# A mixture-of-experts stage whose token lists are made earlier and whose shared MLP is packed into three products instead of four

## The chip, the cores and the metric

One NeuronCore of a Trainium2 chip runs the kernel; the metric is the device time of one execution in microseconds (us), lower is better. TensorE (PE), VectorE (DVE), ScalarE (ACT), GpSimd (POOL) and SyncE (SP) each take their own instructions in program order and wait for each other by semaphores.

## The reference, cut to what matters

The program is a two-layer block over x of 32 batches of 128 tokens of 128 features: attention, an expert layer with 64 experts, attention with a bias, an expert layer with 8 experts. The change touches the first expert layer only. With xf the 4096 normalised tokens:

```python
scores = softmax(xf @ gate_w.T)
_, idx = top_k(scores + gate_b, 6)                # 6 of 64 experts
# each expert takes its first 64 tokens (CAP = 64) of a sorted list
h  = silu(einsum('ecd,eid->eci', xb, w1)) * einsum('ecd,eid->eci', xb, w3)
yb = einsum('eci,edi->ecd', h, w2)                # inner width 88
y  = zeros_like(xf).at[tok].add(contrib * wf[:, None])
z  = silu(xf @ ws1.T) * (xf @ ws3.T) @ ws2.T      # shared MLP, inner width 176
return y + z
```

## The kernel before, in words

The stage is `experts0_block`. It runs between the two attention stages, from about 279 to 388 us of the span. It handles the 64 experts in NG = 8 groups g of GE = 8, and the shared MLP in NB = 8 blocks b of four batches (512 tokens). The order of the work on each engine is written out by hand, as calls of small helpers, and one pass of `for g in range(NG)` is called a turn here.

Helpers on TensorE. `running_counts` and `FIRST` count, with bf16 products, how many tokens each expert has got so far. `picks(n)` (L1204) multiplies kept counts `cumb` by a 0/1 matrix `tile_of`, for half of a group, into the bank PICK; it waits for `l_tiles` of its group (n // 2 + 1), for `l_cumb`, and until DVE has counted what the bank held before. `hidden(b, c)` (L1214) makes the inner rows of the shared MLP: for each half c of 88 inner rows one product of `ws1` and one of `ws3`, each 88x512. `project(b)` (L1226) multiplies by `ws2`. `places(g)` (L1237) transposes the gathered token rows, `expert_hidden(g)` (L1247) makes the 16 inner products of the group's experts, `outputs(g)` (L1259) its eight output products.

On ScalarE, `silu` (L1301) serves the shared MLP, L1310 copies the transposed rows (`xpT`), L1314 is the experts' own silu. On VectorE, `tiles(g)` (L1353 to L1358) builds `tile_of` of a group and releases `picks`, `keep_counts(j)` (L1344) fills `cumb`, `count(n)` (L1369) reads PICK and sums, `tokens(g)` (L1375) turns the sums of a group into addresses, `weights_and_rows(g)` (L1391 to L1395) takes the weights and row numbers out of the gathered rows, `gated(b, half)` (L1329) and L1434 multiply by the silu, `add_shared(b)` (L1334) adds the shared result, `scale(g)` (L1402) weights the experts' outputs. On GpSimd, `fetch(g)` (L1161) issues four indirect DMAs that gather the token rows of a group, `place(g)` (L1172) four that scatter its results. GpSimd's order is fetch(0), fetch(1), and then in turn g: fetch(g + 2), place(g). SP loads the experts' weights.

Lists are made LISTS = 3 groups ahead: in turn g VectorE runs `tiles(g + 3)` right after `weights_and_rows(g)`, and TensorE the two `picks` of that group, one behind `hidden(g + 2, 0)` and one behind `hidden(g + 2, 1)`. The shared MLP is AHEAD = 2 blocks ahead. The turn's first part on TensorE reads

```python
places(g)
if g + AHEAD - 1 < NB:
    project(g + AHEAD - 1)
expert_hidden(g)
if g + AHEAD < NB:
    hidden(g + AHEAD, 0)
if g + LISTS < NG:
    picks(2 * (g + LISTS))
outputs(g)
```

The weights of the shared MLP come with the list `later` in `setup_block`, whose loads SP issues at L403 near 17 us.

Of the kernel before, what the change touches and what calls it, by code (L numbers as in the profile page):

```python
# [178 lines left out]
def setup_block(nc, t, d, sem, ps):  # L179
# [14 lines left out]
        (t.wvT[1], d.wvT1), (t.woT[1], d.woT1), (t.wrT, d.wrT), (t.hs, d.hs), (t.ws13T, d.ws13T), (t.ws2T, d.ws2T),  # L194
# [897 lines left out]
def experts0_block(nc, t, d, sem, ps):  # L1092
# [26 lines left out]
    LISTS = 3  # L1119

# [12 lines left out]
    def pair(n):  # L1133
        return H1[n % 2], H3[n % 2]
# [6 lines left out]
    with nc.Block(no_gpsimd_drain=True) as block:  # L1141
# [45 lines left out]
        def _(pe):  # L1187
# [21 lines left out]
            def hidden(b, c):  # L1209
                n = use(b, c)  # L1210
                free(pe, n)
                rhs = t.XT[:, T4 * b:T4 * b + T4, :].rearrange("p k q -> p (k q)")
                for k, bank in enumerate(pair(n)):
                    mm = nc.tensor.matmul(bank[0:I0, :], t.ws13T[:, (2 * k + c) * I0:(2 * k + c + 1) * I0], rhs,  # L1214
                                          start=True, stop=True)
                mm.then_inc(s_h, 1)

            def project(b):
                if b == 0:
                    pe.wait_ge(l_cumb, 3)  # L1220
                else:
                    pe.wait_ge(s_zadd, b)
                pe.wait_ge(s_u, 2 * b + 2)
                for k in range(T4):
                    for c in range(2):
                        mm = nc.tensor.matmul(Z[:, D * k:D * k + D], t.uT[:, c, S * k:S * k + S],  # L1226
                                              t.ws2T[:, c, :], start=(c == 0), stop=(c == 1))
                mm.then_inc(s_z, 1)
# [39 lines left out]
            hidden(0, 0)  # L1268
            picks(0)
            picks(1)  # L1270
            pe.wait_ge(l_cumb, 1)
            hidden(0, 1)
            hidden(1, 0)
            picks(2)
            picks(3)
            project(0)
            hidden(1, 1)
            picks(4)
            picks(5)
            for g in range(NG):  # L1280
                places(g)
                if g + AHEAD - 1 < NB:
                    project(g + AHEAD - 1)
                expert_hidden(g)
                if g + AHEAD < NB:
                    hidden(g + AHEAD, 0)
                if g + LISTS < NG:
                    picks(2 * (g + LISTS))
                outputs(g)
                if g + AHEAD < NB:  # L1290
                    hidden(g + AHEAD, 1)
                if g + LISTS < NG:
                    picks(2 * (g + LISTS) + 1)

        @block.scalar
        def _(act):
            def silu(b, c):
                n = use(b, c)
                act.wait_ge(s_h, 2 * b + c + 1)
                free(act, n)  # L1300
                nc.scalar.activation(t.silu[:, n % 2, :], pair(n)[0][0:I0, :], ACT.Silu).then_inc(s_e, 1)  # L1301

            for b in range(AHEAD):
                silu(b, 0)
                silu(b, 1)
            for g in range(NG):
                act.wait_ge(r_T, g + 1)
                if g >= 2:
                    act.wait_ge(r_h, g - 1)
                nc.scalar.activation(t.xpT[:, g % 2, :], TP[:, :], ACT.Copy).then_inc(r_Tc, 1)  # L1310
                n = last_uses[g]
                act.wait_ge(r_h, g + 1)
                free(act, n)
                nc.scalar.activation(t.silu[:, n % 2, :], pair(n)[0][0:I0, :], ACT.Silu).then_inc(r_e, 1)  # L1314
                if g + AHEAD < NB:
                    silu(g + AHEAD, 0)
                    silu(g + AHEAD, 1)

        @block.vector
        def _(dve):  # L1320
# [3 lines left out]
            def gated(b, half):  # L1324
# [4 lines left out]
                ve.tensor_tensor(t.uT[:, half, :], pair(n)[1][0:I0, :], t.silu[:, n % 2, :], ALU.mult).then_inc(s_u, 1)  # L1329
# [84 lines left out]
            counted_tokens(0)  # L1414
            gated(0, 0)
            gated(0, 1)
            keep_counts(2)
            tiles(1)
            keep_counts(3)
            counted_tokens(1)  # L1420
            tiles(2)
            gated(1, 0)
            gated(1, 1)
            add_shared(0)
            counted_tokens(2)
            for g in range(NG):
# [5 lines left out]
                if g >= 2:  # L1432
                    dve.wait_ge(r_y, g - 1)
                ve.tensor_tensor(t.gT[:, g % 2, :], pair(n)[1][0:I0, :], t.silu[:, n % 2, :],  # L1434
                                 ALU.mult).then_inc(r_u, 1)
# [12 lines left out]
            c.end()  # L1448
# [422 lines left out]
def flamingo_kernel(nc, **dram):  # L1871
# [41 lines left out]
    with ExitStack() as ctx:  # L1913
# [27 lines left out]
        with ExitStack() as ex0:  # L1941
            t.ws13T = tile(ex0, "ws13T", [4 * I0], F32)
            t.gateT = tile(ex0, "gateT", [E0], F32)
            t.wrT = tile(ex0, "wrT", [E1], F32)
            t.silu = tile(ex0, "silu", [2, 512], F32, I0)
            t.uT = tile(ex0, "uT", [2, 512], F32, I0)
            t.gT = tile(ex0, "gT", [2, 512], F32, I0)
            t.ws2T = tile(ex0, "ws2T", [2, D], F32, I0)
# [199 lines left out]
```

## Time and profile before

| | |
|---|---|
| median of 3 runs | 928.5 us (928.15 to 934.57) |
| span of the profiled execution | 930.0 us |
| TensorE busy in the span | 716.6 us (77%) |
| VectorE busy | 691.5 us (74%) |
| GpSimd busy | 615.0 us (66%) |
| mean granted TensorE clock | 0.910 |

The runs' list does not say which of them was profiled. The span lies 1.5 us above the median; steps are worked out on the span and carried over to the median as differences. In a timeline row the two numbers in front are start and duration in us, and the bracket at the end gives the engine's idle time before the row and what ended it. A merged row (x16) starts with its first instruction. A matmul of f32 shows as two records.

### The profile page before, as it was taken

The page shows a single profiled execution, that of the slowest core. Times are in us where ns is not written, and L with a number is a line of the kernel's source. Part 1 is how long each engine was busy: PE and PEld are TensorE (multiplying, and loading weights), DVE is VectorE, ACT ScalarE, POOL GpSimd, SP SyncE. Part 2 cuts the span into 40 slices and gives each one's busy share as a digit, 9 for nine tenths or more (in the row PEclk, how much of TensorE's full clock was granted, in tenths as well). Part 3 has the DMA queues.
Part 4 walks back from the last instruction along what each step waited for, and adds up shares of the span by engine and source line. Part 5 has one row for each costly group of instructions (what it writes and reads, how often), then busy time and mean ns, then how long its engine had stood idle before and what let it go on. Part 6 is the DMA issues. An engine that isn't in the chain of part 4 may idle for free. (4 is left out here: it accounts for less than half of the span.)

```text
span 930.0 us, 23773 instructions
## 1 busy us (share of the span) xinstructions
PE 716.6 (77%) x6259; PEld 491.8 (53%) x6259; DVE 691.5 (74%) x2257; ACT 473.2 (51%) x1687; POOL 615.0 (66%) x1109
## 2 busy tenths in 40 slices
PE   3888999999947998258999999999711379879770
PEld 1555566556623666236666666666501256567550
DVE  3787999999966664148999999999878756765334
ACT  2886888888831222037777777777500033423220
POOL 4888666666643676467888888887300466777772
PEclk9999999999977999679999999999955599999895
DMA  5211222222113333134344434443100216655568
GB/s 164 77 50 69 78 76 78 79 79 92 71 59 102 105 105 104 47 103 136 126 145 134 132 124 139 143 143 106 59 9 1 81 48 173 179 163 166 163 180 240
DMA packets 98731, 100.61 MB, mean 108 GB/s; under 512 B 24511, under 2 KB 76077, under 8 KB 98659
## 3 DMA queue, kind: packets, MB, share of 16 engines
q1 hardware_dynamic: 88306, 88.25, 30.5%
q0 software_dynamic: 6656, 9.66, 3.7%
q10 hardware_dynamic: 3696, 1.84, 0.7%
q8 instruction: 32, 0.52, 0.2%
q14 instruction: 41, 0.33, 0.1%
HBM read 60.84 MB, written 44.17 MB: 113 GB/s over the span
## 5 line engine op out<-in xcount | busy, mean ns | idle before, releaser
L574 ACT ACTIVATE P<-bank,mx 128x120 f32<-128x120 f32 x1024 | 277.5, 430 | 70.3 <-DVE mx L876 70.3
L473 PE MATMUL bank<-ident,P 128*120 128x128 f32 x1024 | 167.2, 286 | 28.7 <-ACT P L574 24.0
L473 PEld LDWEIGHTS bank<-ident,P 128*120 128x120 f32 x1024 | 106.1, 138 | 116.7 <-issue 70.7
L876 DVE TENSOR_REDUCE mx<-bank 128x4 f32<-128x480 f32 x256 | 150.3, 649 | 21.2 <-PE bank L455 18.1
L1761 POOL DMA_INDIRECT xg<-token_rows,tokens x64 | 66.8, 1044 | 70.8 <-DVE tokens L1815 51.9
L446 PE MATMUL bank<-bp,identr 128*128 128x480 f32 x256 | 87.5, 428 | 0.0
L1771 POOL DMA_INDIRECT expert_sums<-y,sum_rows x64 | 72.8, 1137 | 22.2 <-issue 19.2
L491 PE MATMUL bank<-PT,Vb 120*32 120x128 f32 x2048 | 82.9, 280 | 5.1 <-DVE PT L884 4.5
L676 POOL TENSOR_TENSOR Km<-Kf,kmask 128x480 f32<-128x480 f32 x64 | 63.2, 987 | 28.2 <-ACT Kf L558 27.4
L641 POOL TENSOR_TENSOR rstd<-rs,minus_half 128x1 f32<-128x1 f32 x128 | 73.1, 571 | 10.7
L455 PE MATMUL bank<-Km,qf 32*128 32x480 f32 x512 | 70.9, 623 | 3.0 <-POOL Km L676 2.9
L884 DVE TENSOR_SCALAR PT<-bank,kept 120x512 f32<-120x512 f32 x96 | 67.5, 729 | 0.2 <-PE bank L473 0.2
L1743 ACT ACTIVATE ge<-bank,b1x 128x512 f32<-128x512 f32 x64 | 44.0, 687 | 45.6 <-PE bank L1695 45.6
L1707 PE MATMUL bank<-w2x,ge 128*128 128x128 f32 x512 | 67.1, 288 | 0.0
L1736 ACT ACTIVATE xgT<-bank 128x512 f32<-128x512 f32 x16 | 8.9, 595 | 113.9 <-PE bank L1684 113.9
L640 POOL TENSOR_SCALAR rs<-mv 128x1 f32<-128x1 f32 x128 | 29.1, 227 | 54.8 <-DVE mv L852 54.7
L491 PEld LDWEIGHTS bank<-PT,Vb 120*32 120x32 f32 x2048 | 48.6, 109 | 30.3 <-DVE PT L884 17.6
L1707 PEld LDWEIGHTS bank<-w2x,ge 128*128 128x128 f32 x512 | 63.7, 202 | 1.4 <-issue 1.4
L582 ACT ACTIVATE PT<-bank 120x512 f32<-120x512 f32 x64 | 41.6, 650 | 44.7 <-PE bank L473 44.7
L1695 PE MATMUL bank<-xgT,w1x 128*128 128x512 f32 x128 | 58.6, 611 | 0.0
L882 DVE COPY PT<-bank 120x512 f32<-120x512 f32 x64 | 43.0, 672 | 10.6 <-PE bank L473 10.3
L1161 POOL DMA_INDIRECT xp<-token_rows,place_tok x32 | 33.0, 1030 | 25.4 <-DVE place_tok L1375 16.6
(244 smaller groups left out, 1678.7 us busy)
## 6 DMA issues: line engine op xcount, KB each, us to landing
expert_sums<-zeros SPq DMA_DIRECT2D x32, 512.0 KB, 3.4
choice_rows<-zeros SPq DMA_DIRECT2D x32, 384.0 KB, 2.4
yrows<-choice_rows SPq DMA_DIRECT2D x32, 384.0 KB, 3.1
XT<-expert_sums SPq DMA_DIRECT2D x16, 512.0 KB, 6.3
XS<-expert_sums SPq DMA_DIRECT2D x16, 512.0 KB, 6.1
w<-in_w13T SPq DMA_DIRECT2D x8, 704.0 KB, 4.2
token_rows<-payload SPq DMA_DIRECT2D x32, 128.0 KB, 1.7
ctx<-in_ctxT SPq DMA_DIRECT2D x64, 60.0 KB, 2.0
```

What stands on the lines that cost most here:

```text
L446: nc.tensor.matmul(heads(SC[r]), t.identb[:] if L == 0 else t.identr[:], part.unsqueeze(1).broadcast_to([S, G, KV]), start=(x == 0), stop= ...
L455: nc.tensor.matmul(heads(SC[r]), t.qf[rows, u, :], t.Km[rows, u, :, :], start=False, stop=True).then_inc(ev.scores, 1)
L473: mm = nc.tensor.transpose(TB[r % 2][0:KV, S * j:S * j + S], t.P[:, r, j, :], t.ident[:])
L491: mm = nc.tensor.matmul(pv_ps[32 * j:32 * j + 32, S * (r // 2):S * (r // 2) + S], t.Vb[0:KV, v, 2 * j + r // 2, 32 * (r % 2):32 * (r % 2) ...
L574: e = nc.scalar.activation(t.P[:, r, j, :], heads(SC[r])[:, j, :], ACT.Exp, bias=t.mx[:, G * r + j:G * r + j + 1], scale=-1.0)
L641: power = nc.gpsimd.tensor_tensor(t.rstd[:, k, u, :], t.rs[:, k, u, :], t.minus_half[:], ALU.pow)
L676: nc.gpsimd.tensor_tensor(t.Km[:, w, :, :], t.Kf[:, w, :].unsqueeze(1).broadcast_to([D, G, KV]), t.kmask[:].unsqueeze(2).broadcast_to([D, ...
L876: ve.tensor_reduce(t.mx[:, G * r:G * r + G], heads(SC[r]), AX.X, ALU.min).then_inc(ev.mins, 1)
L884: ve.tensor_scalar(t.PT[0:KV, r, :], TB[r % 2][0:KV, :], at_col(t.kept, i), None, ALU.mult).then_inc(ev.pt_dve, 1)
L1707: mm = nc.tensor.matmul(Y[s][:, D * k:D * k + D], t.ge[:, s, c, 128 * k:128 * k + 128], t.w2x[:, e % 2, c, :], start=(c == 0), stop=(c == ...
L1761: nc.gpsimd.indirect_dma_start(out=t.xg[:, e % 2, k, :], out_offset=None, in_=d.rows_flat, in_offset=bass.IndirectOffsetOnAxis(ap=t.tokens ...
L1771: nc.gpsimd.indirect_dma_start(out=d.sums_flat, out_offset=bass.IndirectOffsetOnAxis(ap=t.sum_rows[:, e, k:k + 1], axis=0), in_=t.y1[:, e ...
```

## The change

Three parts, all in or for `experts0_block`.

First, the packing. The 176 inner rows of the shared MLP are cut into 128 and 48 instead of 88 and 88. `hidden(b, 0)` makes 128 rows of ws1 and 128 of ws3, `hidden(b, 1)` makes the other 48 of both in a single product of 112 rows (the second 48 at row 64). `silu`, `gated` and `project` follow; the second `gated` reads rows 64 to 111 and writes rows 0 to 47. The loads of `ws13T` and `ws2T` become seven DMAs instead of two.

Second, the start. The lists of groups 0, 1 and 2 are made ahead of most of the shared MLP, on TensorE and on VectorE.

Third, the turn. `project(g + 1)` moves behind `expert_hidden(g)`, `hidden(g + 2, 0)` behind `outputs(g)`, the first `picks` of a turn to a place between `places(g)` and `expert_hidden(g)`, the second between the two `hidden`. VectorE's `count`, `scale` and `gated` are put in another order in the turn; `tiles(g + 3)` stays behind `weights_and_rows(g)`.

```diff
-        ... (t.ws13T, d.ws13T), (t.ws2T, d.ws2T),
+        (t.ws13T[:, 0:128], d.ws13T[:, 0:128]), (t.ws13T[:, 128:256], d.ws13T[:, SI:SI + 128]),
+        (t.ws13T[:, 256:320], d.ws13T[:, 128:192]), (t.ws13T[:, 320:368], d.ws13T[:, SI + 128:2 * SI]),
+        (t.ws2T[0:I0, 0, :], d.ws2T[:, 0, :]), (t.ws2T[I0:128, 0, :], d.ws2T[0:128 - I0, 1, :]),
+        (t.ws2T[0:SI - 128, 1, :], d.ws2T[128 - I0:I0, 1, :]),
...
+    REST, UP = SI - 128, 64
...
-                for k, bank in enumerate(pair(n)):
-                    mm = nc.tensor.matmul(bank[0:I0, :], t.ws13T[:, (2 * k + c) * I0:(2 * k + c + 1) * I0], rhs,
+                if c == 0:
+                    for k, bank in enumerate(pair(n)):
+                        mm = nc.tensor.matmul(bank[:, :], t.ws13T[:, 128 * k:128 * k + 128], rhs, start=True, stop=True)
+                else:
+                    mm = nc.tensor.matmul(pair(n)[0][0:UP + REST, :], t.ws13T[:, 256:256 + UP + REST], rhs,
...
             for g in range(NG):
                 places(g)
+                if g + LISTS < NG:
+                    picks(2 * (g + LISTS))
+                expert_hidden(g)
                 if g + AHEAD - 1 < NB:
                     project(g + AHEAD - 1)
-                expert_hidden(g)
+                outputs(g)
                 if g + AHEAD < NB:
                     hidden(g + AHEAD, 0)
                 if g + LISTS < NG:
-                    picks(2 * (g + LISTS))
-                outputs(g)
+                    picks(2 * (g + LISTS) + 1)
                 if g + AHEAD < NB:
                     hidden(g + AHEAD, 1)
-                if g + LISTS < NG:
-                    picks(2 * (g + LISTS) + 1)
```

VectorE's queue in a turn (the one line that stays, `tiles`, is left in to show its place):

```diff
                 weights_and_rows(g)
                 if g + LISTS < NG:
                     tiles(g + LISTS)
...
                                  ALU.mult).then_inc(r_u, 1)
+                if g + LISTS < NG:
+                    count(2 * (g + LISTS))
                 if g + AHEAD - 1 < NB:
                     add_shared(g + AHEAD - 1)
+                scale(g)
                 if g + AHEAD < NB:
                     gated(g + AHEAD, 0)
-                scale(g)
-                if g + LISTS < NG:
-                    count(2 * (g + LISTS))
-                if g + AHEAD < NB:
-                    gated(g + AHEAD, 1)
                 if g + LISTS < NG:
                     count(2 * (g + LISTS) + 1)
                     tokens(g + LISTS)
+                if g + AHEAD < NB:
+                    gated(g + AHEAD, 1)
```

TensorE before, one turn (g = 1), from the transposes on; `tile_of` is the 0/1 matrix that `tiles` makes:

```order
548 L1237 MATMUL bank<-ident,xp 128x128 [waits mlp_places_T_copied,rows_fetched1]
549 L1237 MATMUL bank<-ident,xp 128x128 x3
550 L1226 MATMUL bank<-ws2T,uT 128x128 [waits mlp_gated,mlp_added]
551 L1226 MATMUL bank<-ws2T,uT 128x128 x7
552 L1247 MATMUL bank<-xpT,w 88x64 [waits mlp_weights_loaded1,mlp_places_T_copied,mlp_gated]
553 L1247 MATMUL bank<-xpT,w 88x64 x15
554 L1214 MATMUL bank<-XT,ws13T 88x512 [waits mlp_gated]
555 L1214 MATMUL bank<-XT,ws13T 88x512
556 L1204 MATMUL bank<-cumb,tile_of 128x129 [waits list_counted,list_counts_kept,list_tiles]
557 L1204 MATMUL bank<-cumb,tile_of 128x129
558 L1259 MATMUL bank<-w,gT 64x128 [waits mlp_expert_scaled,mlp_out_weights_loaded1,mlp_expert_gated]
```

The same turn in the changed kernel, whose line numbers are larger (L1246 is the transposes, L1209 `picks`, L1256 `expert_hidden`, L1235 `project`, L1268 `outputs`, L1220 `hidden(b, 0)`):

```order
545 L1246 MATMUL bank<-ident,xp 128x128 [waits mlp_places_T_copied,rows_fetched1]
546 L1246 MATMUL bank<-ident,xp 128x128 x3
547 L1209 MATMUL bank<-cumb,tile_of 128x129 [waits list_counted,list_counts_kept,list_tiles]
548 L1209 MATMUL bank<-cumb,tile_of 128x129
549 L1256 MATMUL bank<-xpT,w 88x64 [waits mlp_weights_loaded1,mlp_places_T_copied,mlp_gated]
550 L1256 MATMUL bank<-xpT,w 88x64 x15
551 L1235 MATMUL bank<-ws2T,uT 128x128 [waits mlp_gated,mlp_added]
552 L1235 MATMUL bank<-ws2T,uT 128x128 x7
553 L1268 MATMUL bank<-w,gT 64x128 [waits mlp_expert_scaled,mlp_out_weights_loaded1,mlp_expert_gated]
554 L1268 MATMUL bank<-w,gT 64x128 x7
555 L1220 MATMUL bank<-XT,ws13T 128x512 [waits mlp_gated]
```

The `picks` with its wait on `list_tiles` has moved ahead of `expert_hidden`, and `project` and `outputs` now stand between `expert_hidden` and the next `hidden`.

VectorE in the changed kernel, from the first `gated` of block 3 in turn 1 to `tile_of` of turn 2; L1341 and L1343 are the two `gated`, L1384 `count`, L1390 `tokens`, L1406 to L1410 `weights_and_rows`, L1368 to L1373 `tiles`:

```order
487 L1341 TENSOR_TENSOR uT<-bank,silu 128x512 [waits mlp_out,mlp_silu]
488 L1384 TENSOR_SCALAR place_junk,place_tokf<-bank,place_rank 128x128 [waits list_picked]
489 L1384 TENSOR_SCALAR place_junk,place_tokf<-bank,place_rank 128x128
490 L1390 TENSOR_SCALAR place_tok<-place_tokf 128x4 [waits list_counted]
491 L1343 TENSOR_TENSOR uT<-bank,silu 48x512 [waits mlp_out,mlp_silu]
492 L1406 COPY wt<-xp 64x4 [waits rows_fetched2]
493 L1407 SCALAR_TENSOR_TENSOR place_rowf<-place_tokf,xp 64x4
...
497 L1368 TENSOR_TENSOR from_first<-slotno,tile_first 128x128
498 L1369 TENSOR_TENSOR to_last<-slotno,tile_last 128x128
499 L1373 SCALAR_TENSOR_TENSOR tile_of<-from_first,same,to_last 128x2x64 [waits vector_chain]
```

Against before, the second `gated` has moved from ahead of `count` and `tokens` to behind them, and `tiles` still stands behind all of these.

## Rows read from the trace of the kernel before

**Rows 1.** The page: the span, and one group of products of 128x512.
```profile
span 930.0 us, 23773 instructions
...
L1695 PE MATMUL bank<-xgT,w1x 128*128 128x512 f32 x128 | 58.6, 611 | 0.0
```
**Rows 2.** Timeline of TensorE over one turn (start, duration, instruction, idle before).
```profile
322.50 0.61 PE L1237 MATMUL bank<-ident,xp 128*128 128x128 f32 x4
324.05 2.02 PE L1226 MATMUL bank<-ws2T,uT 88*128 88x128 f32 x16 [0.94 <-DVE uT L1329]
325.91 2.65 PE L1247 MATMUL bank<-xpT,w 128*88 128x64 f32 x32
328.40 1.90 PE L1214 MATMUL bank<-XT,ws13T 128*88 128x512 f32 x4
...
330.34 1.09 PE L1259 MATMUL bank<-w,gT 88*64 88x128 f32 x16
331.37 1.95 PE L1214 MATMUL bank<-XT,ws13T 128*88 128x512 f32 x4
...
334.81 2.02 PE L1226 MATMUL bank<-ws2T,uT 88*128 88x128 f32 x16 [0.94 <-DVE uT L1329]
```
**Rows 3.** Timeline of GpSimd: first and last scatters, and one turn.
```profile
311.59 1.03 POOL L1172 DMA_INDIRECT choice_rows<-yo,place_row  x1 [2.51 <-DVE yo L1402]
...
331.59 1.00 POOL L1161 DMA_INDIRECT xp<-token_rows,place_tok  x1 [0.30 <-issue]
333.07 1.02 POOL L1172 DMA_INDIRECT choice_rows<-yo,place_row  x1 [0.48 <-issue]
...
375.53 0.98 POOL L1172 DMA_INDIRECT choice_rows<-yo,place_row  x1 [5.28 <-DVE yo L1402]
...
382.86 0.98 POOL L1172 DMA_INDIRECT choice_rows<-yo,place_row  x1 [2.49 <-DVE yo L1402]
```
**Rows 4.** Timeline of ScalarE: the silu behind the product of 331.37.
```profile
333.35 0.59 ACT L1301 ACTIVATE silu<-bank 88x512 f32<-88x512 f32 x1 [2.43 <-PE bank L1214]
```
**Rows 5.** Timeline of VectorE: the end of the first list, and one turn.
```profile
287.64 0.17 DVE L1375 TENSOR_SCALAR place_tok<-place_tokf 128x4 uint32<-128x4 f32 x1
...
333.98 0.69 DVE L1329 TENSOR_TENSOR uT<-bank,silu 88x512 f32<-88x512 f32 x1 [1.06 <-ACT silu L1301]
334.59 0.40 DVE L1369 TENSOR_SCALAR_CACHE_REDUCE place_junk<-bank,place_rank 128x128 f32<-128x128 f32 x1
...
335.45 0.15 DVE L1391 COPY wt<-xp 64x4 f32<-64x4 f32 x1
...
336.09 0.28 DVE L1353 TENSOR_TENSOR from_first<-slotno,tile_first 128x128 bf16<-128x128 f32 x1
...
336.61 1.26 DVE L1358 SCALAR_TENSOR_TENSOR tile_of<-from_first,same,to_last 128x128 bf16<-128x128 bf16 x4
339.99 0.69 DVE L1434 TENSOR_TENSOR gT<-bank,silu 88x512 f32<-88x512 f32 x1 [2.11 <-ACT silu L1314]
```
**Rows 6.** Timeline of SP: one load of the list `later`.
```profile
16.49 0.43 SPq L403 DMA_DIRECT2D ws13T<-in_ws13T  x1
```
**Rows 7.** Timeline of TensorE: after idle stretches, and a slow `outputs`.
```profile
302.01 0.27 PE L1204 MATMUL bank<-cumb,tile_of 128*128 128x129 bf16 x2 [2.71 <-DVE place_junk L1369]
...
379.41 1.93 PE L1259 MATMUL bank<-w,gT 88*64 88x128 f32 x16 [1.40 <-DVE gT L1434]
...
413.48 0.31 PE L422 MATMUL bank<-ident,xn 128*128 128x128 f32 x1 [3.21 <-DVE xn L871]
```
**Rows 8.** Windows: busy us of PE, PEld, DVE, ACT, POOL, then granted clock, DMA share, GB/s.
```profile
301.00:302.00 1.00, 0.00 (x0) 0.02 (x1) 0.86 (x5) 0.00 (x0) 0.69 (x2) 1.00 0.09 17
...
413.00:414.00 1.00, 0.52 (x3) 0.55 (x4) 0.34 (x1) 0.00 (x0) 0.84 (x3) 0.82 0.00 0
414.00:415.00 1.00, 1.00 (x6) 0.93 (x5) 0.48 (x2) 0.23 (x1) 1.00 (x3) 0.50 0.00 0
...
417.00:418.00 1.00, 1.00 (x12) 0.39 (x5) 0.29 (x1) 0.00 (x0) 0.00 (x0) 0.97 0.06 16
```

More of the change, by code:

```diff
@@ L1225, in project @@
                     for c in range(2):
-                        mm = nc.tensor.matmul(Z[:, D * k:D * k + D], t.uT[:, c, S * k:S * k + S],
-                                              t.ws2T[:, c, :], start=(c == 0), stop=(c == 1))
+                        rows = 128 if c == 0 else REST
+                        mm = nc.tensor.matmul(Z[:, D * k:D * k + D], t.uT[0:rows, c, S * k:S * k + S],
+                                              t.ws2T[0:rows, c, :], start=(c == 0), stop=(c == 1))
                 mm.then_inc(s_z, 1)
@@ L1300, in silu @@
                 free(act, n)
-                nc.scalar.activation(t.silu[:, n % 2, :], pair(n)[0][0:I0, :], ACT.Silu).then_inc(s_e, 1)
+                if c == 0:
+                    nc.scalar.activation(t.silu[:, n % 2, :], pair(n)[0][:, :], ACT.Silu).then_inc(s_e, 1)
+                else:
+                    nc.scalar.activation(t.silu[UP:UP + REST, n % 2, :], pair(n)[0][0:REST, :], ACT.Silu).then_inc(s_e, 1)
             for b in range(AHEAD):
@@ L1313, in _ @@
                 free(act, n)
-                nc.scalar.activation(t.silu[:, n % 2, :], pair(n)[0][0:I0, :], ACT.Silu).then_inc(r_e, 1)
+                nc.scalar.activation(t.silu[0:I0, n % 2, :], pair(n)[0][0:I0, :], ACT.Silu).then_inc(r_e, 1)
                 if g + AHEAD < NB:
@@ L1328, in gated @@
                     dve.wait_ge(s_z, b)
-                ve.tensor_tensor(t.uT[:, half, :], pair(n)[1][0:I0, :], t.silu[:, n % 2, :], ALU.mult).then_inc(s_u, 1)
+                if half == 0:
+                    ve.tensor_tensor(t.uT[:, 0, :], pair(n)[1][:, :], t.silu[:, n % 2, :], ALU.mult).then_inc(s_u, 1)
+                else:
+                    ve.tensor_tensor(t.uT[0:REST, 1, :], pair(n)[0][UP:UP + REST, :], t.silu[UP:UP + REST, n % 2, :],
+                                     ALU.mult).then_inc(s_u, 1)
             def add_shared(b):
@@ L1414, in _ @@
             counted_tokens(0)
+            tiles(1)
+            keep_counts(2)
+            counted_tokens(1)
             gated(0, 0)
+            keep_counts(3)
+            tiles(2)
+            count(4)
             gated(0, 1)
[L1417 to L1421, printed above, removed]
+            count(5)
+            tokens(2)
             gated(1, 0)
+            add_shared(0)
             gated(1, 1)
-            add_shared(0)
-            counted_tokens(2)
             for g in range(NG):
@@ L1941, in flamingo_kernel @@
         with ExitStack() as ex0:
-            t.ws13T = tile(ex0, "ws13T", [4 * I0], F32)
+            t.ws13T = tile(ex0, "ws13T", [3 * 128 - 16], F32)
             t.gateT = tile(ex0, "gateT", [E0], F32)
             t.wrT = tile(ex0, "wrT", [E1], F32)
-            t.silu = tile(ex0, "silu", [2, 512], F32, I0)
-            t.uT = tile(ex0, "uT", [2, 512], F32, I0)
+            t.silu = tile(ex0, "silu", [2, 512], F32)
+            t.uT = tile(ex0, "uT", [2, 512], F32)
             t.gT = tile(ex0, "gT", [2, 512], F32, I0)
-            t.ws2T = tile(ex0, "ws2T", [2, D], F32, I0)
+            t.ws2T = tile(ex0, "ws2T", [2, D], F32)
             t.w13 = tile(ex0, "w13", [2, 8, 2 * I0], F32)
```

15 lines of the change are left out of this document (7 added, 8 removed).

## The prediction

> **What bounds the kernel now.** I read the page first and found the stage by its lines, then the timeline of each engine over one turn of the expert loop, then the waits of its last turns, and last the granted clock in narrow windows. The span is 930.0 us [rows 1]; the change touches the roughly 110 us from 279 to 388.
>
> The turn repeats to the hundredth. TensorE starts `project` at 324.05 and again at 334.81 [rows 2], so a turn is 10.76 us. In it TensorE idles 0.94 us, in front of `project`, for VectorE's second `gated`. That wait closes a loop: the last product of a turn starts at 331.37 and ends at 333.32, its silu runs at 333.35 [rows 4], `gated` at 333.98 [rows 5], `project` at 334.81. So TensorE's own order sets the turn: 9.8 us of work and one short wait.
>
> GpSimd is nearly as full. Its last fetch of a turn starts at 331.59 and ends at 332.59, the first scatter at 333.07, a gap of 0.48 where its usual gap is 0.30 [rows 3]. With the usual gap its turn would be 10.76 - 0.18 = 10.58 us. However much shorter TensorE's turn gets, GpSimd takes back all but 0.2 us of it while the loop runs. From the first scatter at 311.59 on, GpSimd has eight scatters and five fetches of groups, 13 x 10.58 / 2 = 68.8 us, and would end at 380.4. It ends near 388 (the last group begins at 382.86, four instructions of 1.3 each) because the results of groups 6 and 7 come late: it idles 5.28 us before 375.53 and 2.49 before 382.86 [rows 3]. The 7 us in the tail are what a better order could win.
>
> **The change, part by part.**
>
> *Packing.* Each block has three products where it had four. One product of 512 columns is half of 1.90 us, 0.95 [rows 2]. A product of 128 rows should cost like one of 88: 128x512 products elsewhere run at 611 ns a record [rows 1], against 4 records in 1.90 here when they follow each other; bounds 0 and +0.2 us a product, I take 0, as what streams is the same 512 columns. TensorE's work in a turn falls from 9.8 to 8.9 us. VectorE and ScalarE keep their instruction counts; the half with 48 rows has the same 512 elements in a row, so 0.69 and 0.59 stay. The five more loads cost SP 5 x 0.47 = 2.4 us of issue near 17 us (a row of 0.43 and its gap) [rows 6]. What is queued behind them is a load for batch 2, which TensorE takes up only when it has been through batches 0 and 1, so I count 0; if that cover failed, it would be 2.4 us.
>
> *The turn.* This part decides. The first `picks` now stands ahead of `expert_hidden(g)` and waits for `list_tiles` of group g + 3. VectorE makes those tiles behind `weights_and_rows(g)`, which stands behind both `gated` and `tokens` of the turn before. Before, the tiles were made while TensorE ran `project` and `expert_hidden`; here everything on TensorE is queued behind that wait: `expert_hidden`, `project`, `outputs` and the next `hidden`, and on `hidden` waits the silu, on that `gated`, on that the next tiles. So a new loop closes. Link by link, from the end of `hidden(g + 2, 0)`:
>
> - to the start of `gated`, by way of the silu: 333.98 - 333.32 = 0.66 [rows 2, 5]
> - first `gated`: 334.59 - 333.98 = 0.61; second `count` and `tokens`: 335.45 - 334.59 = 0.86; second `gated`, again 0.61; `weights_and_rows`: 336.09 - 335.45 = 0.64; `tiles`: 336.09 to 337.87 = 1.78 [rows 5]
> - semaphore and `picks`: about 0.3
> - `expert_hidden`: 328.40 - 325.91 = 2.49; `project`: 325.91 - 324.05 = 1.86; `outputs`: 331.37 - 330.34 = 1.03; `hidden(g + 3, 0)`: 1.90 [rows 2]
>
> The sum is 12.74 us against 10.76, +2.0 a turn. The gap in which TensorE stands still, between `places` (0.61 [rows 2]) and `picks`, is the turn less its work: 12.74 - 8.9 = 3.8 us. The wait exists in turns 0 to 4 (g + 3 < 8), which makes four full turns between the outputs of groups 0 and 4: +8.0.
>
> *The start.* The first list is done at 287.64 and its addresses go to GpSimd; after it VectorE now goes straight on with lists. By the durations above (tiles 1.7, a kept count 0.6, the two counts of a list some 2.3 with their picks between) the lists of groups 1 and 2 come at about 292 and 298. That gives GpSimd its fetches without a pause, but what the first scatter waits for is group 0's result, and its path is now longer: `project(0)`, both `gated`, `add_shared`, `weights_and_rows(0)`, `tiles(3)` all stand ahead of the `picks` that hides `expert_hidden(0)`. Adding them from 298, `expert_hidden(0)` starts at about 304.4 to 305, and it is followed by `project(1)` before `outputs(0)` where `hidden(2, 0)` stood before. The first scatter stays at 311.6 or slips by up to 1: +0.5. The earlier lists win nothing, since nobody waits for them.
>
> *The tail.* In turns 5 to 7 there are no lists and no wait for tiles. `project` now fills the time of the silu between `expert_hidden` and `outputs`. A turn is transposes, their copy, `expert_hidden`, `project`, `outputs` and 1.5 `hidden`: 0.61 + 0.85 (0.59 as for a silu [rows 4], and two handovers) + 2.49 + 1.86 + 1.03 + 2.8 = 9.6 us, and two such replace two of at most 10.76: -2.3 at most, I take -2.0.
>
> With TensorE's clock as before the sum is +0.5 + 8.0 - 2.0 = +6.5 us.
>
> *The clock.* After 2.71 us without work TensorE's clock still stood at 1.00, full 2.4 GHz, at 302 [rows 7, 8]. After 3.21 us, up to 413.48, it fell to 0.50, which is 1.2 GHz, in the window of 413, and came back in that of 417 [rows 7, 8]. It was also slow at 379.41, after a stretch of short pieces of work: `outputs` took 1.93 there against 1.09 [rows 2, 7]. The new gaps of 3.8 us, one in each of five turns, are longer than the one that made it fall. Then `expert_hidden`, `project` and `outputs`, 5.4 us of the new loop, begin slow. In the one short slow stretch that these rows show, 413.6 to 417.0, TensorE was busy throughout, and at half speed such 3.4 us cost 1.6. If all the three ran at the ratio of `outputs`, 1.93 / 1.09 = 1.77, it would be 4.1. I take 2.2 a turn, nearer to the measured stretch: 5 x 2.2 = +11.
>
> The Trainium skill (TensorE: Matmul & The Clock Gate, section HAM oscillation) describes just this: a wait between bursts of products that throttles the clock anew in every iteration, so that each burst starts slow. By that rule the sum is +17.5, without it +6.5. The trace agrees as far as it goes, with the fall after 3.21 us and none after 2.71; a gap of 3.8 us in a repeating loop it does not show.
>
> **Sum.** +0.5 + 8.0 - 2.0 + 11 = +17.5 us, 947.5 on the profiled span, 946 on the median of 928.5.
>
> **Rivals.**
>
> *The clock holds.* The same loop, no fall: 928.5 + 6.5 = 935. For it: TensorE's work between the gaps is dense, and at 302 a gap went by unpunished. Against: the new gap is longer than either of those. If the tail gives a little more, this lies inside 1%.
>
> *The clock does not come back in the loop.* TensorE's part of the loop, 7.3 us, runs wholly slow: 7.3 x 0.77 = 5.6 a turn, five turns +28 and some in the tail; 928.5 + 6.5 + 28 = 963. For it: at 379.41 the clock was down after a wait of only 1.40 [rows 7]. Against: a full burst brought it back at 417 [rows 8].
>
> *GpSimd sets the pace and the change pays.* If `tiles` were ready in time, TensorE would have 8.9 us in a turn, GpSimd 10.58, and GpSimd would run through from 311.6 to 380.4 instead of 388: -7.3, or 921. It decides once TensorE's loop is below 10.58 us, which needs the tiles 2.2 us sooner than the links above give them. For it: GpSimd's fullness. Against: VectorE's row order, where `tiles` stands behind `tokens` and both `gated`.
>
> **How the numbers follow.** Clock falls and recovers, 0.72: 946, its own range 940 to 955. Clock holds, 0.14: 935. Clock stays down, 0.09: 963. GpSimd paces, 0.05: 921. The range of 935 to 959 holds the first with the unknown of 1.6 to 4.1 a turn, takes in the clock-holds case, and leaves out the others. A measurement of this kernel can tell about 1% from no change, which is 9.3 us. Faster by over 1% only if GpSimd paces and nearly all of it comes off, 0.03; within 1% if that is partial or the clock holds, 0.15; slower 0.82.
>
> **What would show it right or wrong.** The timeline should show, in turns 0 to 4, TensorE idle 3.5 to 4.2 us in front of the `picks` behind `places`, released by `tile_of`; `project` without its wait of 0.94; turns of 12.7 us where the clock is full and near 15 where it falls; the granted clock at 0.50 several times between 305 and 375; GpSimd's wait for `yo` in every turn instead of at the end only; the last scatter at about 405 instead of 388. A turn near 10.6 us, or tiles that wait for TensorE rather than the other way round, would prove the second loop wrong. The attention stages should keep their length to within 1 us.

## The result and the profile after

The median of four runs is 985.2 us (984.5 to 988.5), against 929.0 us for the kernel before in the same comparison. The ratio of the runs is 1.0557, with a 95% interval of 1.051 to 1.0603: slower by 5.6%. (It is not the quotient of the two medians, which lie 56.2 us or 6.0% apart.) The forecast was 946, with a range of 935 to 959. It had the direction and less than a third of the size: 17.5 of some 56 us.

In three of the sets of runs below every kernel took some 40 to 75 us longer, the kernel before too (1003 to 1006 us, against 929 to 937 in the others), so each ratio is taken against the kernel before in its own set, and a slow set is named as such.

The page of the profiled execution: its first line, the busy times, and the granted clock in 40 slices (in tenths, 9 is 90% or more):

```profile
span 986.8 us, 23746 instructions
PE 757.8 (77%) x6243; PEld 520.7 (53%) x6243; DVE 693.6 (70%) x2257; ACT 473.4 (48%) x1687; POOL 613.1 (62%) x1109
PEclk9999999999955676766999999999975569999995
```

The span is 56.8 us longer than in [rows 1]. TensorE is busy 41 us more than before (716.6) although it has fewer products, so its products got slower. VectorE and GpSimd are busy as long as before, within some 2 us. The clock row puts the slow part into slices 12 to 19 (each is 24.7 us), all but the last of them the expert stage, and there it does not get back to 9.

TensorE over one turn, the counterpart of [rows 2]. L1246 is `places`, L1209 `picks`, L1256 `expert_hidden`, L1235 `project`, L1268 `outputs`, L1220 and L1222 the two `hidden`. The row says only "128*128" for `project` because it is named by its first record; 8 of its 16 records have 48 rows.

```profile
345.14 0.60 PE L1246 MATMUL bank<-ident,xp 128*128 128x128 f32 x4
349.73 0.29 PE L1209 MATMUL bank<-cumb,tile_of 128*128 128x129 bf16 x2 [3.99 <-DVE tile_of L1373]
349.85 4.29 PE L1256 MATMUL bank<-xpT,w 128*88 128x64 f32 x32
353.93 5.80 PE L1235 MATMUL bank<-ws2T,uT 128*128 128x128 f32 x16
359.67 1.97 PE L1268 MATMUL bank<-w,gT 88*64 88x128 f32 x16
361.57 3.27 PE L1220 MATMUL bank<-XT,ws13T 128*128 128x512 f32 x4
364.68 0.28 PE L1209 MATMUL bank<-cumb,tile_of 128*128 128x129 bf16 x2
364.79 1.06 PE L1222 MATMUL bank<-XT,ws13T 128*112 128x512 f32 x2
365.69 0.60 PE L1246 MATMUL bank<-ident,xp 128*128 128x128 f32 x4
370.36 0.29 PE L1209 MATMUL bank<-cumb,tile_of 128*128 128x129 bf16 x2 [4.07 <-DVE tile_of L1373]
```

Read the brackets first. TensorE stands still for 4 us ahead of `picks`, released by `tile_of`: the wait of the forecast, which put it at 3.8. `project` has lost its own wait of 0.94. But a turn takes 370.36 - 349.73 = 20.63 us, where 10.76 stood before and 12.7 to 15 was forecast. The durations say why: `expert_hidden` takes 4.29 (2.65 in [rows 2]), `project` 5.80 (2.02), `outputs` 1.97 (1.09), two products of `hidden` 3.27 (1.90).

Stretches of two such turns (mean over the stretch; behind the busy times stand the granted clock, the DMA share and GB/s):

```profile
350.00:364.00 14.00, 14.00 (x68) 10.62 (x67) 2.80 (x7) 0.59 (x1) 2.96 (x4) 0.52 0.25 70
364.00:371.00 7.00, 2.93 (x19) 1.57 (x18) 4.54 (x18) 1.78 (x3) 5.27 (x6) 0.99 0.10 31
371.00:385.00 14.00, 14.00 (x64) 10.49 (x63) 2.80 (x7) 0.59 (x1) 3.01 (x3) 0.51 0.28 77
```

TensorE works for 14 us without a pause at 0.51 or 0.52, that is, nearly all of it at 1.2 GHz. It gets 2.4 GHz back for the 7 us in which it is busy for 2.9, and falls again. In windows of 1 us the clock still reads 1.00 through the whole wait, up to 350, and 0.50 from 351 on, when the work has resumed. TensorE has the fast clock when it doesn't need it.

GpSimd's own idle time moved as forecast, from the end of the stage [rows 3] into every turn:

```profile
342.58 1.02 POOL L1177 DMA_INDIRECT choice_rows<-yo,place_row  x1 [10.37 <-DVE yo L1417]
...
363.21 1.02 POOL L1177 DMA_INDIRECT choice_rows<-yo,place_row  x1 [10.43 <-DVE yo L1417]
...
383.98 1.02 POOL L1177 DMA_INDIRECT choice_rows<-yo,place_row  x1 [10.58 <-DVE yo L1417]
```

And the waits between 276 and 446 us, summed (us in all, times, longest). The largest, GpSimd's and ScalarE's, are consequences: both wait for TensorE's results. The row that starts it is the last shown, TensorE's wait for `tile_of`.

```profile
POOL choice_rows L1177 <- DVE yo L1417: 74.1, 8, 17.9
ACT silu L1310 <- PE bank L1220: 69.0, 8, 10.3
...
PE bank L1209 <- DVE tile_of L1373: 22.1, 6, 4.2
```

The starts of `outputs` cut the loss into three: the first comes at 318.4 (308.8 before), +9.6; from there four turns take 83.05 us (43.05), +40.0; the last three 33.9 (27.5), +6.3. Together +55.9 of the 56.8, so the stages behind lost under 1 us.

Three things are then to be told apart: the wait itself, the slow clock, and `project`, whose 5.80 is more than twice 2.02.

### The profile page after: what moved, and what is told of

Read it like the earlier page. It is cut to its first block and busy times, and to the rows that moved or that the text cites. A ratio compares the mean times of both kernels' runs of the same rounds, so it can differ in the third digit from the quotient of the medians.

```text
span 986.8 us, 23746 instructions
## 1 busy us (share of the span) xinstructions
PE 757.8 (77%) x6243; PEld 520.7 (53%) x6243; DVE 693.6 (70%) x2257; ACT 473.4 (48%) x1687; POOL 613.1 (62%) x1109
## 5 line engine op out<-in xcount | busy, mean ns | idle before, releaser
L1177 POOL DMA_INDIRECT choice_rows<-yo,place_row x32 | 31.7, 991 | 81.4 <-DVE yo L1417 74.1
```

## The experiments

In the slow sets differences came out far smaller (the changed kernel is at 1.0248 there, and at 1.0557 in the other), so the readings here rest on the other sets. Turns are read from the starts of `outputs`. A "point" is 1% of the time of the kernel before. Durations and spans are of one profiled execution of each kernel.

### The tiles one group earlier

```diff
+            tiles(3)
...
             for g in range(NG):
...
-                if g + LISTS < NG:
-                    tiles(g + LISTS)
+                if g + LISTS + 1 < NG:
+                    tiles(g + LISTS + 1)
```

Nothing is taken off TensorE; its wait alone goes.

> The changed kernel with tile_of built one group earlier on VectorE, once more, since on the first chip of the experiments even the kernel before took 1006 us and the silu behind expert_hidden started up to 4 us after the last product's modelled end. Theory on a chip where before takes 929 us: no wait for tile_of, turns of about 11.5 us at the full clock, about 932 us. Rival: packing or order keep the clock low: turn above 16 us, time above 960.

Measured: 940.5 us, ratio 1.0084 [1.0027, 1.014]. The timeline of TensorE:

```profile
339.32 0.60 PE L1246 MATMUL bank<-ident,xp 128*128 128x128 f32 x4
340.64 0.27 PE L1209 MATMUL bank<-cumb,tile_of 128*128 128x129 bf16 x2 [0.72 <-DVE place_junk L1384]
340.83 2.69 PE L1256 MATMUL bank<-xpT,w 128*88 128x64 f32 x32
343.35 3.36 PE L1235 MATMUL bank<-ws2T,uT 128*128 128x128 f32 x16
346.64 1.86 PE L1268 MATMUL bank<-w,gT 88*64 88x128 f32 x16
```

The wait for `tile_of` is gone and 4.7 points of the 5.6 with it; the loop's turns are 11.2 and 12.8 us alternately. So the wait is the cause of most of the loss, directly or through the clock. The time is 8 us over the 932 expected. Two things are left: `project` takes 3.36 us even at the full clock, and in every second turn the clock still dips (`outputs` at 1.86 here), though no gap of TensorE in these turns is over 0.72 us.

### The gap filled with work, the wait kept

```diff
                 places(g)
                 if g + LISTS < NG:
+                    pe.wait_ge(l_counted, 4 * (g + LISTS))
+                    for _ in range(13):
+                        nc.tensor.matmul(PICK[:, 384:512], t.ident[:], t.ident[:], start=True, stop=True)
                     picks(2 * (g + LISTS))
```

The products go to columns of the bank that nobody reads. This keeps the loop through `tile_of` and takes away only TensorE's idleness in it.

> The changed kernel with 13 products filled into the wait of each turn, once more. Theory on a chip where before takes 929 us: the clock stays full in the loop, turn about 14 us, about 950 us. Rival: the clock falls all the same, turn 20 us, 985 or above.

Measured, in two runs of 951.0 and 959.6 us: median 955.3 us, 1.0212 [1.0097, 1.0328], span 949.3.

```profile
332.82 3.17 PE L1293 MATMUL bank<-ident 128*128 128x128 f32 x26 [0.63 <-DVE place_junk L1387]
336.27 0.29 PE L1209 MATMUL bank<-cumb,tile_of 128*128 128x129 bf16 x2 [0.28 <-DVE tile_of L1376]
336.39 2.67 PE L1256 MATMUL bank<-xpT,w 128*88 128x64 f32 x32
338.89 3.36 PE L1235 MATMUL bank<-ws2T,uT 128*128 128x128 f32 x16
342.18 1.09 PE L1268 MATMUL bank<-w,gT 88*64 88x128 f32 x15
```

And its clock in the loop, beside the changed kernel's:

```profile
305.00:400.00 95.00, 87.41 (x693) 67.57 (x694) 44.66 (x145) 16.03 (x27) 47.71 (x48) 1.00 0.26 77
```
```profile
305.00:400.00 95.00, 75.96 (x358) 55.67 (x359) 33.29 (x117) 10.54 (x18) 32.27 (x32) 0.64 0.21 60
```

Thirteen useless products a turn (26 records) make the kernel faster by 3.4 points, and the clock holds at 1.00 through the loop. With two runs the size is known to about a point either way; the two intervals, 1.0097 to 1.0328 and 1.051 to 1.0603, do not touch. From the end of `places` (332.2) to `picks` (336.3) pass the same 4.1 us as in the changed kernel, so the wait has not changed; the turn is 14.44. What the slow clock costs is thus 20.63 - 14.44 = 6.2 us a turn. The durations of four steps account for it: 4.29 + 5.80 + 1.97 + 3.27 = 15.33 against 2.67 + 3.36 + 1.09 + 1.98 = 9.10.

### Even rows in both halves of `project`, padded

```diff
+        ... (t.ws2T[SI - 128:128, 1, :], d.ws2T[0:80, 0, :]),
...
+                    const.then(nc.gpsimd.memset(t.uT[:, 1, :], 0.0))
...
-                        rows = 128 if c == 0 else REST
-                        mm = nc.tensor.matmul(Z[:, D * k:D * k + D], t.uT[0:rows, c, S * k:S * k + S],
+                        mm = nc.tensor.matmul(Z[:, D * k:D * k + D], t.uT[0:128, c, S * k:S * k + S],
...
```

The second product of each pair has 128 rows like the first, 80 of them zeros in `uT`; `ws2T` is read with 128 rows too (left out above). It does more work on paper and the same number of products.

> The changed kernel with 128 rows in both halves of project, once more. The first chip showed the padded project but its times are not comparable. Theory where before takes 929 us: project 2.0 full and about 3.7 slow, turn about 18.3, time about 971. Rival: project stays at 3.35 and 5.8, time 985.

Measured, in two runs: 955.1 us, 1.0211 [1.0162, 1.0259]. Padding with zeros takes away 3.5 points, more than was expected (971 us).

```profile
335.97 0.29 PE L1210 MATMUL bank<-cumb,tile_of 128*128 128x129 bf16 x2 [4.06 <-DVE tile_of L1373]
336.10 4.78 PE L1256 MATMUL bank<-xpT,w 128*88 128x64 f32 x32
340.67 3.14 PE L1235 MATMUL bank<-ws2T,uT 128*128 128x128 f32 x16
343.74 1.09 PE L1268 MATMUL bank<-w,gT 88*64 88x128 f32 x16
```
```profile
330.00:343.00 13.00, 8.94 (x55) 7.87 (x53) 5.89 (x23) 2.38 (x4) 8.12 (x8) 0.74 0.19 50
343.00:353.00 10.00, 5.94 (x45) 3.83 (x45) 5.97 (x20) 1.78 (x3) 5.11 (x5) 1.00 0.26 84
```

The wait is the same 4.06 and the clock still falls, but it is back before `outputs` (1.09, full clock), where in the changed kernel it comes back only at the end of `hidden`. This turn and its neighbour take 16.2 and 16.3 us, the other two 14.7 and 17.1. A mean of 0.74 over 13 us means (1 - 0.74) / 0.5 x 13 = 6.8 us at half clock, half of the 14 of the changed kernel. The mixed rows thus cost twice: by themselves, and in a longer slow stretch behind the same wait. Why the stretch is shorter with padded rows is not shown; the next kernel has equal rows too, and there it is 10 to 12 us.

### The new order with the old packing

Four products of 88 rows for a block and `project` with 88 and 88 rows, as before the change, in the order of the changed kernel.

> The changed order with the unpacked shared MLP, once more. Theory where before takes 929 us: project as before, the wait for tile_of near 3.5 us, clock still falling, turn about 18.5 us, time about 972. Rival: the packing costs nothing, 985 to 988.

Measured, in two runs: 972.1 us, 1.0391 [1.0344, 1.0438], as expected; turns of 18.8 us, 3.29 us of wait ahead of `picks`, the clock at 0.68 between 305 and 400. With equal rows `project` takes 3.73 us even in the slow stretch, against 5.80. The order alone is therefore a loss of 3.9%, about 37 us; packing with 128 and 48 rows on top makes it 5.6%.

The same four kernels (tiles early, gap filled, padded, old packing) ran first in a slow set, where they gave 1.0026, 1.0158, 1.0022 and 1.0142, each within 0.4% either way. They lie closer together than in the other sets, and no size is read from them.

### Forty-eight rows in both halves

```diff
-                        rows = 128 if c == 0 else REST
+                        rows = REST
```

On top of the filled gap. It leaves out 80 of the first 128 inner rows in `project`, so the shared MLP's result is incomplete; all else is computed.

> The kernel with the filled gap, whose clock stays full and whose project takes 3.36 us, with 48 rows in both halves of project (the shared MLP's first 128 inner rows count only 48 of them, 80 are left out). Theory: what costs is the change of the row count between one product and the next; with 48 everywhere project is back near 2.0 us and the turn near 13.1. Rival: a product of 48 rows is slow by itself; then project stays at 3.4 or gets longer.

Measured: 941.0 us against 937.3, 1.0053 [1.0021, 1.0084]; the turn is 13.24 us where 13.1 was expected. The records of `project` (128 of them; minimum, median and maximum in ns, first and last start, shapes), here and in the kernel with the filled gap, which differ in the number of rows alone:

```profile
L1235 PEld LDWEIGHTS bank<-ws2T,uT x128: 182/188/188, 297.4 to 381.5; 48*128 48x128 f32 x128
L1235 PE MATMUL bank<-ws2T,uT x128: 272/272/373, 297.4 to 381.6; 48*128 48x128 f32 x128
```
```profile
L1235 PEld LDWEIGHTS bank<-ws2T,uT x128: 182/187/193, 298.1 to 393.0; 128*128 128x128 f32 x64, 48*128 48x128 f32 x64
L1235 PE MATMUL bank<-ws2T,uT x128: 272/302/378, 298.1 to 393.1; 128*128 128x128 f32 x64, 48*128 48x128 f32 x64
```

With 48 rows in both the 16 records take 2.05 us, with 128 and 48 in turn 3.36, with 128 in both 2.00 (below). The 48 rows cost nothing; that neighbours differ does. The load's own record is nearly as long in all three: 188, 187 and 192 ns in the median. The turn of 13.24 us at the full clock is what the new order costs with the wait in it and neither the slow clock nor the long `project`: 2.5 over 10.76.

### The packing alone

The kernel before, in its old order, with the packing of the changed one.

> The kernel before, order untouched, with the three-product packing alone. Theory: the second hidden is 0.9 us shorter, project 1.3 longer, no gap is added and the clock stays full; the turn is 10.76 - 0.9 + 1.3 = 11.2 us, eight turns +3, so 1.003 of before. Rival: the 48-row products themselves lower the clock, as they lengthen the slow stretches in the changed kernel; then the clock shows 0.50 in the loop and the ratio is above 1.01.

Measured: 953.8 us, 1.0176 [1.0122, 1.023], where 1.003 was expected. A part that looks harmless, one product fewer in a block, costs 1.8% by itself. Turns at the full clock are 11.5 us, `project` 3.4. The clock also falls inside the loop and stays low in the tail:

```profile
347.00:354.00 7.00, 7.00 (x39) 6.14 (x39) 1.20 (x4) 0.59 (x1) 5.24 (x6) 0.54 0.09 15
...
385.00:426.00 41.00, 18.57 (x113) 16.23 (x113) 6.96 (x18) 2.85 (x7) 16.18 (x24) 0.50 0.13 38
```

It falls at 347 in the midst of `project`, and no gap of TensorE in the turn before that is over 0.6 us. So a long wait is one way to the slow clock here and not the only one.

The largest part of this kernel's loss lies ahead of the loop, though. Its clock stands at 0.50 from 293 to 316, where that of the kernel before is at 1.00 from 295 to 378:

```profile
293.00:316.00 23.00, 20.27 (x76) 14.67 (x76) 8.52 (x35) 1.78 (x3) 9.13 (x9) 0.50 0.04 7
```
```profile
295.00:378.00 83.00, 72.08 (x606) 53.42 (x606) 48.62 (x173) 16.35 (x28) 54.79 (x54) 1.00 0.31 89
```

The first `outputs` comes at 317.9 instead of 308.8, +9.1 us; the four turns behind it take 49.1 instead of 43.1, +6.0; the last three 34.9 instead of 27.5, +7.4. Of these 22.5 us (from spans of two sets; by the ratio the loss is 16.5) the longer turn at the full clock, 0.7 us over 10.76, makes up some 5. So more of what this kernel lost is slow clock than longer products, and the prediction had no term for that. Only one execution of each was profiled, but the mean clock over the span is 0.889 to 0.892 in all four runs of this kernel and 0.898 to 0.916 in the 23 of the kernel before in its set.

### `picks` behind `project`, with and without padded rows

```diff
                 places(g)
-                if g + LISTS < NG:
-                    picks(2 * (g + LISTS))
                 expert_hidden(g)
                 if g + AHEAD - 1 < NB:
                     project(g + AHEAD - 1)
+                if g + LISTS < NG:
+                    picks(2 * (g + LISTS))
                 outputs(g)
```

The order of the changed kernel, but `expert_hidden` and `project` cover the time in which VectorE makes the tiles.

> The changed kernel with only the first picks of a turn moved behind project; project keeps 128 and 48 rows. Theory: the wait goes, project stays long at 3.35 us, TensorE's work is about 10.3 us a turn, GpSimd and TensorE are about level: a turn near 11, ratio 1.00 within half a per cent. Rival: the place of picks doesn't matter, ratio above 1.02.

> The changed kernel with the first picks of a turn moved from ahead of expert_hidden to behind project, and 128 rows in both halves of project. Theory: nothing waits for tile_of, TensorE's work is 8.9 us a turn, GpSimd's 10.58 sets the pace, and the tail is shorter: 922 to 927 where before takes 929, a ratio near 0.995. Rival: a new wait for the counts takes the place of the old one; ratio 1.00 or above.

Measured: without the padded rows 944.9 us, 1.0093 [1.0061, 1.0126]; with them **925.7 us, 0.9877 [0.9836, 0.9919]**, faster than the kernel before and than the 0.995 expected. One step of TensorE moved and 80 rows of zeros take the changed kernel from 5.6% slower to 1.2% faster. Between the two kernels the first `outputs` differs by 9.1 us (316.6 and 307.5, with the clock at 0.50 from 300 to 319 in the one without padding) and the seven turns by 10.3. TensorE and GpSimd in that version:

```profile
332.77 2.69 PE L1256 MATMUL bank<-xpT,w 128*88 128x64 f32 x32 [0.91 <-issue]
335.29 2.00 PE L1235 MATMUL bank<-ws2T,uT 128*128 128x128 f32 x16
337.13 0.28 PE L1210 MATMUL bank<-cumb,tile_of 128*128 128x129 bf16 x2
337.34 1.09 PE L1268 MATMUL bank<-w,gT 88*64 88x128 f32 x16
```
```profile
369.41 0.98 POOL L1178 DMA_INDIRECT choice_rows<-yo,place_row  x1 [1.46 <-DVE yo L1417]
...
375.92 0.98 POOL L1178 DMA_INDIRECT choice_rows<-yo,place_row  x1 [1.66 <-DVE yo L1417]
...
379.78 0.98 POOL L1178 DMA_INDIRECT choice_rows<-yo,place_row  x1 [0.30 <-issue]
```

No `picks` waits. TensorE's turn is 9.94 us, shorter than the 10.5 that GpSimd needs, so GpSimd runs through and idles only 1.46 and 1.66 us in the tail instead of 5.28 and 2.49 [rows 3]. Its last scatter ends at 380.8 instead of 387.7. This is the rival "GpSimd sets the pace and the change pays": it forecast 380.4 and -7.3 us. The span is 923.5, 6.5 shorter than in [rows 1], though of another set; in its own set the medians lie 11.6 us apart. It is the only set in which this version ran, six times.

### Runs in slow sets that left their question open

Filled gap with padded rows should have given the wait alone, with every row computed; the changed kernel ran once more beside it, with `picks` behind `project` in the old packing and the early tiles with padded rows.

> The changed kernel with the gap filled and 128 rows in both halves of project. Theory: only the wait for tile_of is left; the turn is 13.1 to 13.2 us at the full clock, the ratio about 1.007, 7 us over before. Rival: terms hang together in another way and the ratio stays above 1.015.

> The changed kernel once more, beside the others. Theory: the slow stretches of 13.7 us a turn come back at the same place, ratio 1.05 to 1.06. Rival: they hung on the phase of one run; then the turn is 16 to 18 us and the ratio 1.03.

> The new order with the first picks behind project, and the four-product shared MLP of before. Theory: TensorE's turn is 9.94 + 0.9 = 10.8 us, about that of before, and the tail is short as in the version with three products: ratio 0.990 to 0.997, 2 to 6 us over that version. Rival: the packing wins nothing once project is padded, the ratio is 0.988 as well.

> The changed kernel with tile_of built one group earlier and 128 rows in both halves of project; the first picks stay ahead of expert_hidden. Theory: with neither wait for the tiles nor row change the turn is 10 to 10.6 us and the ratio 0.987 to 0.992. Rival: the picks ahead of expert_hidden wait for the counts instead (0.7 us seen), the clock falls now and then, ratio 0.995 to 1.0.

Measured in a set where the kernel before takes 1003.4: 0.9977 [0.9953, 1.0], 1.0248 [1.0203, 1.0294], 0.9994 [0.9969, 1.002] and 0.9979 [0.9949, 1.001]. The first and third were repeated, again in a slow set (1005.8), with 1.0042 [1.0018, 1.0067] and 1.0021 [0.9995, 1.0048]. The changed kernel is slower there too, though not by the 1.05 to 1.06 expected, and shows the same mechanism: `project` 5.80 and 4.04 us ahead of `picks`.

```profile
354.15 5.80 PE L1235 MATMUL bank<-ws2T,uT 128*128 128x128 f32 x16
...
371.05 0.29 PE L1209 MATMUL bank<-cumb,tile_of 128*128 128x129 bf16 x2 [4.04 <-DVE tile_of L1373]
```

The turns show why less of it reaches the end. In the slow sets the changed kernel's turn is much the same as elsewhere (20.7 to 21.8 us), but the others are long: 15.8 to 16.3 us for `picks` behind `project` in the old packing, 15.6 to 16.2 for the early tiles with padded rows, 15.6 to 17.3 for the filled gap with padded rows; the early tiles alone take 15.7 to 16.3 there, against 11.2 and 12.8 elsewhere. The last `outputs` of the changed kernel starts 25.8 us after that of the old packing (438.8 and 413.1), which is what separates their medians (24.8). So something else sets a turn of about 16 us there, and only what is over it shows. (The kernel before has no profile in a slow set.) One place where it shows is the silu behind `expert_hidden`, here in the old packing:

```profile
339.00 2.69 PE L1248 MATMUL bank<-xpT,w 128*88 128x64 f32 x32 [0.78 <-issue]
...
344.70 0.33 SPq L1149 DMA_DIRECT2D w<-in_w13T  x1
344.71 0.59 ACT L1314 ACTIVATE silu<-bank 88x512 f32<-88x512 f32 x1 [5.81 <-remote]
```

The silu starts 3.0 us after the modelled end of the products, together with SP's load into the buffer of the weights that these products have read; in the best version it starts 0.03 us after that end (335.49). This suggests that the products really ended later than the profile has them; why, and what makes a set slow, is not shown. (A slow set and one that is not carry the same chip number in the record.)

The other three lie within 0.5% of before in both directions, so two questions stay open: the filled gap with padded rows at this kernel's usual time, and how much of the 1.2% of the best version is the packing's and how much the order's.

## Why the prediction was wrong, step by step

The step that failed most is the clock term, 2.2 us a turn or +11 in all, sized by a slow stretch from another place; the second is the packing, put at 0. The kernels can be read as a ladder that gives each its size. The last three columns are what the first `outputs`, the four turns behind it and the last three turns come later or take longer than before. The spans are of kernels in more than one set, so each is good to a few us, and the second kernel leaves 80 rows out.

| kernel | turn, us | span, us | ratio to before | start | four turns | last three |
|---|---|---|---|---|---|---|
| before | 10.76 | 930.0 | 1 | | | |
| changed, gap filled, 48 rows in both | 13.24 | 938.5 | 1.0053 | +0.3 | +9.9 | -1.3 |
| changed, gap filled | 14.44 | 949.3 | 1.0212 | +4.4 | +14.8 | +1.2 |
| changed | 20.6 | 986.8 | 1.0557 | +9.6 | +40.0 | +6.3 |

From rung to rung that is 8.9 us where +6.5 was forecast for order and wait, 11.5 where 0 was forecast for the packing (4.2 of it at the start, where the clock also dips to 0.69 between 300 and 305), and 35.6 where 11 was forecast for the clock: together 56 against 17.5.

**The turn, +2.0 each: right, a little low.** The second loop, through `tile_of`, `picks`, `expert_hidden`, `project`, `outputs` and `hidden`, is there, with a gap of 4.0 to 4.2 us where 3.8 was worked out (3.0 in the first turn), and a turn of 13.24 where 12.74 was: +2.5.

**The start, +0.5, and the tail, -2.0: right for equal rows at the full clock.** With the gap filled and 48 rows in both halves the first `outputs` comes at 309.1, +0.3. In the best version the last three turns take 26.0 us against 27.5, -1.5. In the changed kernel the start costs +9.6 and the tail +6.3, since both also run on a slow clock and with the long `project`. I had put no clock term on the tail and only one turn's on the start.

**The packing, 0: wrong.** The step that failed here is "`project`: 325.91 - 324.05 = 1.86" in the sum of links, taken over as it was, and "what streams is the same 512 columns", weighed for `hidden` alone. `hidden` did as forecast (1.98 for two products of 128 rows). But `project` had become products of 128 and of 48 rows in turn, and takes 3.36 us for 16 records at the full clock instead of 2.0. That is 1.2 us a turn (14.44 - 13.24) and 1.6 points in the ladder; the packing alone costs 1.8%, and more of its loss is slow clock than long products. The Trainium skill (TensorE: Matmul & The Clock Gate, section LDWEIGHTS) says that a load of 32 rows takes as long as one of 128, since the columns count. The trace agrees for the load records: 187 ns in the median with 128 and 48 rows mixed, 188 with 48 alone. From that I would have called the mixed pair free, but the matmul records beside them are longer, 302 against 272 ns in the median.

**The clock, 2.2 a turn: the step that failed most.** It measured 6.2 a turn (20.63 - 14.44), with 5.2 more at the start and 5.2 in the last three turns, 35.6 us where 11 stood; by the ratios it is 3.4 points, some 32 us. The mechanism was forecast, a gap of 3.8 us that makes the clock fall in each turn; the size was not, and it lay outside the bounds of 1.6 to 4.1 too. I took 2.2 as "nearer to the measured stretch" of 3.4 us at 413, in which TensorE did other work. The rows held a closer one: the clock low at 379.41 in just this loop, by which I had priced the rival "does not come back in the loop" at 5.6 a turn, and then gave it 0.09. That rival was nearest in size, and not right as told: the clock does come back in every turn, at 364 to 371, but only behind the work of the loop. It was priced over 7.3 us of work; measured, the slow stretch is some 14 us of each turn, because work at half clock is longer itself, and `project` is longer at both clocks (3.36 and 5.80). The ratio of slow to full came out as 15.33 / 9.10 = 1.68, near the 1.77 of the bound; it was the amount of work that runs slow, 9.1 us at the full clock instead of 5.4, that the bound had too small.

**The terms multiply.** I added the wait, the packing and the clock as if each stood alone. They act on each other: with padded rows the slow stretch of a turn is 6.8 us, with mixed rows 14, after the same gap; and with the gap filled the mixed rows cost 1.6 points, with it open 3.5 (1.0557 against 1.0211). My range of 24 us had no room for that.

**The rivals.** "The clock holds" is what the filled gap does artificially: 955 with the mixed rows, 941 with equal ones (in sets where before takes 934 and 937), against a forecast of 935. "GpSimd paces" needed the tiles 2.2 us sooner; moving `picks` 4.4 us later in TensorE's queue does the same, and with padded rows it then paid at least as priced. Tiles made a group earlier did not pay in the changed kernel (1.0084), where the long `project` and dips of the clock are left.

**The signs.** The wait for `tile_of`, `project` without its own wait, the clock at 0.50 in every turn and GpSimd's wait in every turn came as forecast; turns of 20.6 us where near 15 was named, and a last scatter that ends at 443.7 where 405 was, did not.

## What to carry to other kernels

Before a wait moves ahead of a queue, add up what stands behind it on that engine and whether any of it feeds the signal waited for; here two steps moved ahead of the wait turned a 4 us hole in each turn into none. Where such a hole is on TensorE, price all the work of the turn at its slow durations, from rows of the same loop, and not a short recovery from elsewhere. And when inner rows are cut unevenly for fewer products, look at the products that alternate between the two sizes; padding the smaller to the larger was cheaper here.

## What the runs showed that I had not expected

- Products whose weight loads alternate between 128 and 48 rows: 16 records of `project` in 3.36 us at 2.4 GHz and 5.80 at 1.2 GHz; 2.00 with 128 in both, 2.05 with 48 in both, 2.02 with 88 in both (3.73 in a slow stretch). Why they are longer was not looked into, nor whether other unequal pairs do the same; the load records stay at 187 ns at the full clock.
- How long the slow stretch lasts depends on the work: half clock for 6.8 us of a turn with padded rows, 10 to 12 in the old packing with 88 rows and a fourth product, some 14 with mixed rows, after gaps of 4.06, 3.29 and 3.99 us. What in the work decides it was not tested.
- The clock also falls without a long gap: at 347 in the packing alone, behind a turn whose gaps were 0.6 us at most, and in every second turn with the early tiles, whose gaps are 0.72. What makes it fall there was not tested.
- A slow stretch ahead of the loop can cost as much as all that is in it: the packing alone lost 9.1 us before its first `outputs`, at half clock from 293 to 316.
- 13 useless products a turn made the kernel 3.4 points faster, in two runs.
